# A sequence kernel's front stages rebuilt, and its expert phase issued in another order

## The chip, the cores and the metric

One core of one Trainium2 chip. The metric is device time in microseconds (us) of one execution, lower is better; the value before is a median of three runs. PE is TensorE's matmul stream (PEld its weight loads), DVE is VectorE, ACT ScalarE, POOL GpSimd, and SP SyncE, which issues most transfers.

## The reference

An attention layer with a gated delta rule, then a mixture of experts, each behind a layer norm and with a residual. Shapes: x is 16 x 512 x 256; 16 heads, key width 64, value width 128; 8 experts with an inner width of 32, 2 chosen per token. All in float32.

```python
# attention, x already normed
beta = sigmoid(x @ w_b) * 2
g = -exp(A_log) * softplus(x @ w_a + dt_bias)
q, k, v = (causal_conv_silu(x @ w) for w in (w_q, w_k, w_v))   # 4 taps
q, k = l2norm(q), l2norm(k)
S = S * exp(g_t); delta = (v_t - k_t S) * beta_t                # per step and head
S = S + outer(k_t, delta); o_t = (q_t * DK ** -0.5) S
y = (o * rsqrt(mean(o * o) + 1e-5) * norm_w * silu(x @ w_g)) @ w_out
x = x + layernorm(y)
# experts, on layernorm(x)
V = x @ Wv.T + bv; r = V @ Wg.T + bg; c = sqrt(sum(pv * pv)) / sqrt(8)
s = ln(r) + sigmoid(alpha) * ln(c); w = softmax of the two largest s
x = x + layernorm(V + sum_e w_e * (silu(V @ W1[e].T + b1[e]) @ W2[e].T + b2[e]))
```

## The kernel before

`build` runs these phases in a row; each ends with a barrier of all engines (`Phase.finish`, L102).

1. `make_constants` (L261) builds identity, triangle and block masks on POOL, one instruction after another. PE, DVE and ACT wait for the last of them.
2. `phase_norm` (L315): 16 tiles of 512 tokens. Per tile: load x, statistics (L385), root on POOL (L394), normalize on DVE (L398), eight transposes on PE (L367), two copies on ACT (L375), store to `xT_scratch` (L378), and the gate products with `w_ab` on PE (L341), copied out by DVE (L350). Tiles are staged by one slot each with two buffers.
3. `phase_gates` (L412): loads `w_out`, `norm_w`, `A_log`, `dt_bias`; POOL scales `w_out` (L433) behind clearing the accumulator `acc` (L1142); DVE adds `dt_bias` (L442), ACT takes Abs, Exp and Ln, DVE the maximum (L452) and the product (L454), PE a cumulative sum (L462) and transposes (L472), ACT writes rows (L476), and SP stores them as `g_scratch` and the scaled weights as `wo_scratch`.
4. `phase_delta` (L486): POOL clears and fills `bm`, `m1`, `ktok` (L1106 to L1116), all engines wait for it, then 131 slots. A slot issues stage a (projections, L633, evicted by ACT at L641), stage b (decays: POOL selects from `grow` at L746, ACT takes Exp at L752; inverses) and stage c (recurrence, output, `acc`, L1092) of different blocks. The first 12 slots and the last are written out, the rest is a loop of two slots.
5. `phase_experts` (L1150): 16 tiles of 512 tokens. `body(t)` issues one slot: the steps of all tiles under way, in the order of the table `EXPERT_ORDER` (L74). A name such as `w_T.4` means: step w_T, of the tile that is four slots behind the newest. `issue_slot` (L210) walks the table; each engine gets its own steps in this order and runs them in this order. A step waits for the steps that it reads (`s.need`). After `body(0)`, `compose_weights` (L1249) folds Wv into the router and first expert weights.

The steps of a tile in the experts, in the order of their data:

- x steps: x_bn0, x_mv0, x_ve0 (statistics, L1348, L1326, L1331, DVE), x_rs0 (root, L1334, POOL), x_sh0 (L1337, DVE), x_y1 (normalize, L1316, ACT), x_x1 (residual, L1361, DVE), the same five again as x_bn1 to x_sh1, x_xf (L1316, ACT), x_turn (eight transposes, L1374, PE), x_xT (L1380, ACT).
- q steps: q_mm (router products, L1389, PE), q_b (L1398, DVE), q_sq (ACT), q_c2 (DVE), q_cn (root, L1411, POOL). h steps: h_mm (L1420, PE), h_th, h_z (ACT), h_s (L1434, DVE).
- r steps on DVE: r_sum (L1446), r_cen (L1449), r_cen2, r_var, r_vare, then r_rstd (L1461, POOL), r_n0 (L1465), r_n1, r_score, r_bias. t steps on DVE: t_max, t_idx, t_gap, t_idxf, t_hot, t_den, t_sh0, t_sh1 (L1514), t_w, t_we (L1524), with t_e2 (L1499) on ACT behind t_gap and ahead of t_den.
- w steps: w_turn (L1529, PE), w_T (L1534, ACT), w_V (L1561, PE), w_mm and w_b (L1540, L1545, PE), w_hw (L1551, DVE), w_out (L1567, PE).
- o steps: o_bn (L1573), o_mv, o_ve (DVE), o_rs (POOL), o_sh (DVE), o_n (L1316, ACT), o_sum (L1588, POOL), o_store (SP).

## Time and profile before

| | before |
|---|---|
| median of 3 runs | 5167.19 us (5162.3 to 5168.27) |
| profiled execution, its own time | 5161.75 us |
| its span | 5160.5 us |
| busy: PE, DVE, ACT, POOL | 94%, 81%, 67%, 60% of the span |
| instructions | 151355 |
| DMA | 208.41 MB, mean 40 GB/s |

The span is the time from the first to the last instruction in the profile; the execution's own time is what the runs are measured by. In a timeline row the two numbers at the start are start and duration in us; what stands in brackets is how long the engine had been idle before, and what released it. "x4" means that four instructions are merged in one row. The weight matrices make each float32 product two PE instructions, so a trace counts 16 where the program has 8.

### The profile page before, as it was taken

How to read it: one execution, taken by the hardware profiler on the slowest of the kernel's cores; microseconds unless marked ns; L12 is line 12 of the kernel's file. 1: busy time of each engine (PE TensorE's matmuls, PEld its weight loads, DVE VectorE, ACT ScalarE, POOL GpSimd, SP SyncE). 2: the span in 40 equal slices, each digit the busy share in tenths (PEclk: the TensorE clock that was granted, in tenths of full speed). 3: DMA queues.
4: the chain of work that ended last, by engine and by line, in shares of the span. 5: the costliest groups of instructions: out<-in, count | busy, mean ns of one | idle time of the engine just before them, and what ended most of it. 6: DMA issues, size and time to landing. Idle time of an engine off the chain costs nothing. (4 is left out here: it accounts for less than half of the span.)

```text
span 5160.5 us, 151355 instructions
## 1 busy us (share of the span) xinstructions
PE 4836.9 (94%) x44460; PEld 3853.6 (75%) x44460; DVE 4173.2 (81%) x9991; ACT 3443.0 (67%) x10245; POOL 3110.1 (60%) x4445
## 2 busy tenths in 40 slices
PE   6699999999999999999999999999999999999788
PEld 6477777777777777777777777777777777777566
DVE  5588888888888888888888888888888888887675
ACT  1477776777677776777677767777677777776443
POOL 3566666666666666666666656666566666665465
PEclk9899999999999999999999999999999999999788
DMA  4210111101011010111101111011010110100110
GB/s 147 67 40 32 40 37 39 39 29 43 33 39 39 29 41 36 38 39 33 43 29 39 39 37 39 30 38 45 31 39 30 38 47 29 39 30 20 49 58 33
DMA packets 116478, 208.41 MB, mean 40 GB/s; under 512 B 12418, under 2 KB 70932, under 8 KB 116372
## 3 DMA queue, kind: packets, MB, share of 16 engines
q1 hardware_dynamic: 116372, 207.10, 11.7%
q8 instruction: 53, 0.87, 0.1%
q14 instruction: 53, 0.43, 0.0%
HBM read 187.66 MB, written 19.40 MB: 40 GB/s over the span
## 5 line engine op out<-in xcount | busy, mean ns | idle before, releaser
L648 DVE SCALAR_TENSOR_TENSOR cv<-ps_a,wqkv,cv 128x511 f32<-128x511 f32 (+2 forms) x1536 | 1143.2, 744 | 73.3 <-ACT cv L641 40.1
L633 PE MATMUL ps_a<-xin,wqkv 128*128 128x512 f32 x2048 | 1004.0, 613 | 33.4 <-POOL m L1116 31.1
L852 POOL TENSOR_TENSOR bm<-bat,mask 128x256 f16<-128x256 f32 x1536 | 1032.5, 694 | 0.0
L902 ACT ACTIVATE m<-b 128x256 f16<-128x256 f32 x1536 | 569.2, 388 | 424.7 <-PE b L897 424.6
L913 DVE TENSOR_TENSOR tt<-tt,b 128x256 f16<-128x256 f16 x1536 | 616.0, 415 | 94.8 <-PE b L908 74.5
L955 ACT CAST tt<-bu 128x256 f16<-128x256 f32 x1536 | 572.0, 372 | 134.8 <-PE bu L950 117.1
L1055 POOL TENSOR_TENSOR rms<-msq,epsq 128x2 f32<-128x2 f32 x512 | 99.7, 195 | 920.8 <-ACT sqo L1050 920.8
L633 PEld LDWEIGHTS ps_a<-xin,wqkv 128*128 128x128 f32 x2048 | 363.6, 193 | 292.0 <-issue 285.3
L1087 PE MATMUL ps_a<-wout,yT 128*128 128x256 f32 x2048 | 557.5, 395 | 0.5 <-ACT yT L1081 0.5
L829 DVE SCALAR_TENSOR_TENSOR bat<-ps_a,w,dec 128x256 f32<-128x256 f32 x1024 | 445.3, 476 | 113.7 <-PE ps_a L816 113.7
L897 PEld LDWEIGHTS b<-tt,bm 128*128 128x128 f16 x6144 | 348.8, 98 | 234.6 <-issue 191.8
L780 PE MATMUL ps_b<-wgate,xin 128*128 128x256 f32 x2048 | 504.9, 390 | 0.0
L641 ACT ACTIVATE cv<-ps_a,wqkv 128x512 f32<-128x512 f32 x512 | 352.3, 688 | 174.6 <-PE ps_a L633 174.4
L908 PE MATMUL b<-m,tt 128*128 128x64 f16 x6144 | 421.9, 193 | 32.6 <-ACT m L902 32.5
L950 PE MATMUL bu<-tt,m 128*128 128x64 f16 x6144 | 431.4, 193 | 1.6 <-ACT m L902 0.8
L897 PE MATMUL b<-tt,bm 128*128 128x64 f16 x6144 | 406.3, 193 | 4.4 <-DVE tt L913 3.2
L1092 DVE TENSOR_TENSOR acc<-acc,ps_a 128x256 f32 (+1 forms) x512 | 214.7, 419 | 236.6 <-PE ps_a L1087 235.3
L780 PEld LDWEIGHTS ps_b<-wgate,xin 128*128 128x128 f32 x2048 | 369.5, 190 | 39.1
L816 PE MATMUL ps_a<-kq 64*128 64x256 f32 x2048 | 293.3, 404 | 111.0 <-DVE acc L1092 104.0
L950 PEld LDWEIGHTS bu<-tt,m 128*128 128x128 f16 x6144 | 320.1, 97 | 95.6 <-issue 76.0
L908 PEld LDWEIGHTS b<-m,tt 128*128 128x128 f16 x6144 | 330.2, 98 | 73.7 <-ACT m L902 48.4
L1023 PE MATMUL co<-uu,bat 128*128 128x128 f32 x2048 | 375.2, 275 | 0.0
(223 smaller groups left out, 12447.6 us busy)
## 6 DMA issues: line engine op xcount, KB each, us to landing
xin<-xT_scratch SPq DMA_DIRECT2D x128, 512.0 KB, 3.3
grow<-g_scratch SPq DMA_DIRECT2D x128, 512.0 KB, 4.1
gam<-g_scratch SPq DMA_DIRECT2D x256, 96.0 KB, 2.8
n_x<-in_x SPq DMA_DIRECT2D x16, 512.0 KB, 3.6
xT_scratch<-n_xT SPq DMA_DIRECT2D x16, 512.0 KB, 2.6
e_x<-in_x SPq DMA_DIRECT2D x16, 512.0 KB, 4.2
out_y<-e_yo SPq DMA_DIRECT2D x16, 512.0 KB, 2.9
wqkv<-in_w_qkv SPq DMA_DIRECT2D x32, 128.0 KB, 3.3
```

The costliest lines, as they stand in the source:

```text
L633: ins = pe.matmul(ps[:], wqkv[:, k, j * P:(j + 1) * P], xin[p][:, k, :], start=k == 0, stop=k == KT - 1)
L648: s.done(dve.scalar_tensor_tensor(y[:, r:], ps[:, 0:T - r], tap[:, j, TAPS - 1 - r:TAPS - r], y[:, r:], ALU.mult, ALU.add), f"a_tap{j}{r}")
L780: ins = pe.matmul(ps_b[:, m * 2 * DV:(m + 1) * 2 * DV], xin[p][:, k, t], wg[:, k, :], start=k == 0, stop=k == KT - 1)
L829: ins = dve.scalar_tensor_tensor(bat[:, p:p + 2, u, :], ps[:, n * 2 * P:(n + 1) * 2 * P] .rearrange("p (q t) -> p q t", q=2), col(w1[p], u ...
L852: s.done(pool.tensor_tensor(half_of(bm[:, l, units(g), :], l, 1), half_of(bt[:, units(g), :], l, 1), half_of(c["mask"][:, l, :].unsqueeze( ...
L897: ins = pe.matmul(half_bank(bank, l)[:, k], bm[:, l, u, :], half_of(tt[:, 0], l, 0)[:, u], start=True, stop=True)
L902: s.done(act.mul(half_of(m1[:, l, units(g), :], l, 0), half_bank(bank, l), -1.0), f"b_Me{l}{g}")
L908: ins = pe.matmul(half_bank(bank, l)[:, k], tt[:, 1, u, :], half_of(m1[:, l], l, 0)[:, u], start=True, stop=True)
L913: s.done(dve.tensor_tensor(even, even, half_bank(bank, l), ALU.add), f"b_Ve{l}{g}")
L950: ins = pe.matmul(half_bank(bu, l)[:, k], m1[:, l, u, :], half_of(tt[:, 1], l, 1)[:, u], start=True, stop=True)
L955: s.done(act.copy(half_of(tt[:, 1, units(g), :], l, 1), half_bank(bu, l)), f"b_Ue{l}{g}")
L1087: ins = pe.matmul(ps_a[m % 2][:, 0:D], yT[:, h, :], wo[:, h, :], start=h == 0, stop=h == 1)
```

## The change

- `make_constants` builds only identity, `still`, `half` and `minus_half` at once; the rest, with `bm`, `m1` and `ktok` for delta, comes from a generator that `phase_norm` advances by three steps a slot (`n_build`).
- `phase_norm` is written as steps with lags (`NORM_ORDER`), with four x and xT buffers, two for the others; normalizing goes from DVE to ACT. It also loads `A_log`, `dt_bias`, `norm_w` and `w_out`, scales `w_out` on POOL in eight parts, and stores `wo_scratch` at its end.
- `phase_gates` is gone. Its arithmetic is `decay_gates` in `phase_delta`, in buffers of delta; the first loads of delta are issued ahead of it (`load_first`), the loads of `grow` and `gam` wait for `g_scratch`, which is stored in two halves from ACT's queue.
- `acc` isn't cleared; the first 16 blocks copy into it. 20 delta slots are written out before the loop, not 12.
- `EXPERT_ORDER` is another list, with lags 0 to 3 (19 slots) in place of 0 to 5 (21 slots), and two waits of PE for steps of PE are added.

```diff
--- before.py
+++ after.py
 
 EXPERT_ORDER = """
-    w_turn.4 w_T.4 x_bn0 h_th0.3 w_V0.4 o_sum.5 l_x x_x1.1 w_V1.4 h_s1.4 h_z0.3 x_mv0 x_bn1.1 h_th1.3 h_s0.3
-    r_sum.3 r_cen.3 r_cen2.3 r_var.3 x_ve0 h_z1.3 w_mm.4 r_vare.3 x_xf.2 r_rstd.3 w_hw0.4 w_hw1.4 x_mv1.1 x_rs0
-    x_turn.2 r_n0.3 x_ve1.1 r_n1.3 w_out0.4 r_score.3 x_sh0 r_bias.3 w_out1.4 t_max.3 x_xT.2 o_bn0.4 t_idx.3
-    o_bn1.4 q_mm.2 x_y1 o_store.5 h_mm0.2 t_gap.3 t_idxf.3 o_mv.4 q_b.2 t_e2.3 o_ve.4 q_sq.2 x_rs1.1 t_hot.3
-    t_den.3 t_sh0.3 o_rs.4 q_c2.2 h_mm1.2 t_sh1.3 o_sh.4 t_w.3 o_n0.4 x_sh1.1 q_cn.2 o_n1.4 t_we.3
+    o_bn0.3 o_bn1.3 o_mv.3 o_ve.3 o_rs.3 o_sh.3 o_n0.3 o_n1.3 o_sum.3 o_store.3 t_max.2 t_idx.2 t_gap.2 t_idxf.2
+    t_e2.2 t_hot.2 t_den.2 t_sh0.2 t_sh1.2 t_w.2 t_we.2 w_turn.2 w_V0.2 w_V1.2 w_T.2 w_mm.2 w_hw0.2 w_hw1.2
+    w_out0.2 w_out1.2 q_mm.1 q_b.1 h_mm0.1 h_mm1.1 q_sq.1 h_th0.1 h_z0.1 h_th1.1 h_z1.1 q_c2.1 q_cn.1 h_s0.1 h_s1.1
+    r_sum.1 r_cen.1 r_cen2.1 r_var.1 r_vare.1 r_rstd.1 r_n0.1 r_n1.1 r_score.1 r_bias.1 l_x x_bn0 x_mv0 x_ve0 x_rs0
+    x_sh0 x_y1 x_x1 x_bn1 x_mv1 x_ve1 x_rs1 x_sh1 x_xf x_turn x_xT
 """.split()
...
+    def build_later():
+
+
...
+            step(pool.memset(c["m1"][:, lev, 0, :], 0.0))
+            odd = lambda t: t.rearrange("p u (b k r) -> p u b k r", k=2, r=2 << lev)[:, :, :, 1, :]
+            step(pool.tensor_copy(odd(c["m1"][:, lev, 0:1, :]), odd(c["ident16"][:].unsqueeze(1))))
+            yield
+            step(pool.tensor_copy(c["m1"][:, lev, 1:NU, :], c["m1"][:, lev, 0:1, :].broadcast_to([P, NU - 1, P])))
+            yield
+        for p in range(2):
+            step(pool.memset(c["ktok"][p][:], 0.0))
+            yield
+
     step(pool.memset(c["ident"][:], 1.0))
     step(pool.affine_select(out=c["ident"][:], in_=c["ident"][:], pattern=[[-1, P]], compare_op=ALU.is_equal,
                             fill=0.0, base=0, channel_multiplier=1))
...
+NORM_ORDER = """
+    n_load n_sh.3 n_xT.4 n_bn.2 n_xn.3 n_mv.2 n_ve.2 n_rs.2 n_store.4 n_turn.3 n_ab.4 n_build n_abo.5
+""".split()
+N_LAG = lags_of(NORM_ORDER)
+N_LAGS = max(N_LAG.values())
+BUILD = 3
+
...
+        def loads_later(t):
+
+
+            if t == 0:
+                sp.dma_start(wab[:], w_ab).then_inc(s.sem("n_wab_in"), 16)
...
+        def tile(i):
+            p, q = i % 2, i % NX
+            if (yield "n_load"):
+                s.need(sp, i - NX, "n_xn")
+                s.loaded(sp.dma_start(x_in[q][:], x[i:i + 1].rearrange("a p c d -> p (a c) d")), f"n_x_in{q}")
+            if (yield "n_bn"):
+                dve.wait_ge(s.sem(f"n_x_in{q}"), (i // NX + 1) * 16)
+                s.need(dve, i - 1, "n_mv")
+                for k in range(CH):
+                    ins = dve.bn_stats(stats[:, k, :], x_in[q][:, k, :])
+                s.done(ins, "n_bn")
+            if (yield "n_mv"):
+                s.need(dve, i, "n_bn")
+                s.need(dve, i - 1, "n_sh")
+                settle(dve, c["still"][:, 0:2])
+                for k in range(CH):
+                    ins = dve.bn_aggr(mv[:, k, :], stats[:, k, :])
+                s.done(ins, "n_mv")
+            if (yield "n_ve"):
+                s.need(dve, i, "n_mv")
+                s.need(dve, i - 2, "n_xn")
+                s.done(dve.tensor_scalar(rstd[p][:], mv[:, :, 1], LN_EPS, None, ALU.add), "n_ve")
+            if (yield "n_rs"):
+                s.need(pool, i, "n_ve")
+                s.done(pool.tensor_tensor(rstd[p][:], rstd[p][:], c["minus_half"][:, 0:CH], ALU.pow), "n_rs")
+            if (yield "n_sh"):
+                s.need(dve, i, "n_rs")
...
+                s.need(act, i - 2, "n_turn")
+                for k in range(CH):
+                    ins = act.activation(xn[p][:, k, :], x_in[q][:, k, :], ACT.Identity, bias=shift[p][:, k:k + 1],
+                                         scale=rstd[p][:, k:k + 1])
+                s.done(ins, "n_xn")
+            if (yield "n_turn"):
+                s.need(pe, i, "n_xn")
+                s.need(pe, i - 2, "n_xT")
                 for k in range(KT):
                     for m in range(CH):
...
+                s.need(act, i - NX, "n_ab")
+                if i >= NX:
+                    act.wait_ge(s.sem(f"n_xT_out{q}"), (i // NX) * 16)
                 for k in range(KT):
...
+        def build(t):
+            if (yield "n_build"):
+                for k in range(BUILD):
+                    next(later, None)
+                if t >= NB // 2:
+                    next(scaling, None)
+
+        for t in range(NB + N_LAGS):
+            loads_later(t)
+            threads = [(build(t), 0)]
+            for lag in range(N_LAGS + 1):
+                if active(t - lag, NB):
+                    threads.append((tile(t - lag), lag))
+            issue_slot(N_LAG, threads)
+        for k in later:
+            pass
+        for k in scaling:
+            pass
+        sp.wait_ge(s_ws, NP)
+        sp.dma_start(wo_dram.rearrange("n p h d -> p n (h d)"), wo[:]).then_inc(s_small, 16)
+        for q in range(NX):
+            sp.wait_ge(s.sem(f"n_xT_out{q}"), 16 * NB // NX)
+        sp.wait_ge(s_small, 48)
         ctx.finish()
...
@@ -1089,7 +1094,11 @@
                 if (yield f"c_acc{m}"):
                     s.need(dve, i, f"c_out{m}")
                     a = acc[:, bass.ds((i % NB) * CH + m, 1), :].rearrange("p a d -> p (a d)")
-                    s.done(dve.tensor_tensor(a, a, ps_a[m % 2][:, 0:D], ALU.add), f"c_acc{m}")
+                    if isinstance(i, int) and i < NB:
+                        ins = dve.tensor_copy(a, ps_a[m % 2][:, 0:D])
+                    else:
+                        ins = dve.tensor_tensor(a, a, ps_a[m % 2][:, 0:D], ALU.add)
+                    s.done(ins, f"c_acc{m}")
 
             return [recur()] + [emit(m) for m in range(CH)]
 
-        zero = s.sem("zeroed")
-        pool.memset(bm[:], 0.0).then_inc(zero, 1)
-        pool.memset(m1[:], 0.0).then_inc(zero, 1)
-        pool.memset(still[:], 0.0).then_inc(zero, 1)
-        for p in range(2):
-            pool.memset(ktok[p][:], 0.0).then_inc(zero, 1)
-        pool.wait_ge(zero, 5)
-        for l in range(NLEV):
-            odd = lambda t: t.rearrange("p u (b k r) -> p u b k r", k=2, r=2 << l)[:, :, :, 1, :]
-            ident = c["ident16"][:].unsqueeze(1)
-            for u in range(NU):
-                ins = pool.tensor_copy(odd(m1[:, l, u:u + 1, :]), odd(ident))
-        ins.then_inc(zero, 1)
-        for eng in (pe, act, dve, pool):
-            eng.wait_ge(zero, 6)
-        load_pair(0)
...
+        def load_first():
+
+
+            load_x(0, 0, 0)
+            pair = w_qkv[0:1].rearrange("a p n -> p (a n)")
+            for j in range(4):
+                s.loaded(sp.dma_start(wqkv[:, :, j * P:(j + 1) * P],
+                                      pair[:, 0:KT * N_QKV].rearrange("p (k n) -> p k n", k=KT)[:, :, j * P:(j + 1) * P]),
+                         f"wqkv_in{j}")
+            s.loaded(sp.dma_start(wq[:, KT * N_QKV:], pair[:, KT * N_QKV:]), "tap_in")
+            load_x(1, 1, 1)
+            s.loaded(sp.dma_start(wg[:], w_gate[0:1].rearrange("a p k n -> p (a k) n")), "wg_in")
+            s.loaded(sp.dma_start(wo[:], wo_dram[0:1].rearrange("a p h d -> p (a h) d")), "wo_in")
+            sp.wait_ge(s_out, 32)
+            load_rows(0)
+            load_rows(1)
+            load_x(2, 2, 0)
...
+        def decay_gates():
+
+
+            W = NIT * NU
+            z, az = [tinv[k][:].rearrange("p u t -> p (u t)") for k in range(2)]
+            rows = vtok[0][:]
+            ps = halves
+            at0, at1 = gate_tok[0][:, 0:W], gate_tok[1][:, 0:W]
+            by_head = lambda t: t.rearrange("p (q x h) -> p q x h", q=NP, h=2)
+            spread = lambda t: t.rearrange("p (q x h) -> p q x h", x=1, h=2).broadcast_to([P, NP, W // H, 2])
+            s_v, s_a, s_p = ctx.semaphore("g_dve"), ctx.semaphore("g_act"), ctx.semaphore("g_pe")
+
+            dve.tensor_tensor(by_head(z), by_head(at0), spread(dtb[:]), ALU.add).then_inc(s_v, 1)
+            act.wait_ge(s_v, 1)
...
+            act.activation(az, z, ACT.Abs).then_inc(s_a, 1)
+            act.wait_ge(s_a, 1)
+            act.activation(az, az, ACT.Exp, scale=-1.0).then_inc(s_a, 1)
+            act.activation(alog[:], alog[:], ACT.Exp).then_inc(s_a, 1)
+            act.activation(at1, at1, ACT.Tanh, scale=0.5).then_inc(s_a, 1)
+            act.wait_ge(s_a, 2)
+            act.activation(az, az, ACT.Ln, bias=1.0).then_inc(s_a, 1)
+            dve.wait_ge(s_v, 1)
+            dve.wait_ge(s_a, 5)
+            dve.scalar_tensor_tensor(z, z, 0.0, az, ALU.max, ALU.add).then_inc(s_v, 1)
+            dve.wait_ge(s_v, 2)
+            dve.tensor_tensor(by_head(z), by_head(z), spread(alog[:]), ALU.mult).then_inc(s_v, 1)
+            pe.wait_ge(s_v, 3)
+            for k in range(2):
+                pe.matmul(ps[k][:], c["upper"][:], z[:, k * 512:(k + 1) * 512], start=True, stop=True).then_inc(s_p, 1)
+            dve.tensor_scalar(at1, at1, 1.0, None, ALU.add).then_inc(s_v, 1)
+            for k in range(2):
+                dve.wait_ge(s_p, k + 1)
...
+                act.dma_start(g_dram[k * 512:(k + 1) * 512].rearrange("(a r) t -> r a t", r=P),
+                              rows[:, 4 * k:4 * k + 4, :]).then_inc(s_out, 16)
+            act.wait_ge(s_v, 6)
+            pe.wait_ge(s_a, 7)
+            dve.wait_ge(s_a, 7)
+            pool.wait_ge(s_a, 7)
+            pool.wait_ge(s_v, 6)
+
+        load_first()
         with sp.Fori(1, NP) as hp:
             load_pair(hp)
-        in_slots(nc, NIT, LAGS, 12, COMPUTE, body)
+        decay_gates()
+        in_slots(nc, NIT, LAGS, FIRST, COMPUTE, body)
         ctx.finish()
 
 
...
@@ -1533,7 +1604,7 @@
                 s.need(act, i - 1, "w_b")
                 s.done(act.copy(weT[:], rb[:]), "w_T")
             if (yield "w_mm"):
-                s.need(pe, i, "w_T")
+                s.need(pe, i, "w_T", "w_V1")
                 free(pe, i, "w_mm")
                 for m in range(KT):
                     at = m * HALF
@@ -1561,7 +1632,7 @@
                         ins = pe.matmul(o[j], xT[p][:, k, tok[j]], wv[:, k, :], start=k == 0, stop=False)
                 s.done(ins, f"w_V{half}")
             if (yield f"w_out{half}"):
-                s.need(pe, i, "w_hw0", "w_hw1")
+                s.need(pe, i, "w_hw0", "w_hw1", "w_b")
                 for j in range(2):
                     for k in range(KT):
                         ins = pe.matmul(o[j], hw[p][:, k, tok[j]], w2[:, k, :], start=False, stop=k == KT - 1)
```

What the table moves is seen on two engines, each in one expert slot of the steady state. First DVE, from t_we (L1524) on, in the kernel before:

```order
L1524 TENSOR_TENSOR e_we<-e_hot 128x8x8
L1348 BN_STATS e_stats<-acc 128x6 x4
L1361 TENSOR_TENSOR acc<-acc,e_x 128x1024
L1434 SCALAR_TENSOR_TENSOR e_hw<-e_hth,e_hz 128x512
L258 TENSOR_TENSOR e_still<-e_still 1x1
L1326 BN_AGGR e_mv<-e_stats 128x2 x4
L1348 BN_STATS e_stats<-acc 128x6 x4
L1434 SCALAR_TENSOR_TENSOR e_hw<-e_hth,e_hz 128x512
L1446 TENSOR_REDUCE e_total<-e_rv 128x8
L1449 SCALAR_TENSOR_TENSOR e_rv<-e_rv,e_total 128x64
L1452 TENSOR_TENSOR e_cen<-e_rv 128x64
L1455 TENSOR_REDUCE e_var<-e_cen 128x8
```

and in the changed kernel, where t_we is L1595, t_sh1 L1585, w_hw L1622, q_b L1469 and L1470, q_c2 L1478, h_s L1505 and r_sum L1517:

```order
L1582 RECIPROCAL e_share<-e_share 128x4
L1585 TENSOR_TENSOR e_share<-e_share,e_e 128x4
L1589 TENSOR_TENSOR e_hot<-e_hot,e_share 128x32 x2
L1595 TENSOR_TENSOR e_we<-e_hot 128x8x8
L1622 TENSOR_TENSOR e_hw<-e_hw,e_t 128x512 x2
L1469 TENSOR_TENSOR e_rv<-e_rb,e_rowb 128x4x8
L1470 TENSOR_TENSOR e_pv<-e_rb,e_rowb 128x256
L1478 TENSOR_REDUCE e_c<-e_pv 128x32
L1505 SCALAR_TENSOR_TENSOR e_hw<-e_hth,e_hz 128x512 x2
L1517 TENSOR_REDUCE e_total<-e_rv 128x8
```

Between t_we and w_hw there stood thirteen rows of other steps; now none does, and none between w_hw and q_b. PE in one slot, before (w_turn L1529, w_V L1561, w_mm L1540, w_b L1545, x_turn L1374, w_out L1567, q_mm L1389, h_mm L1420):

```order
L1529 MATMUL e_rb<-ident,e_we 128x128 x4
L1561 MATMUL e_ob<-e_wv,e_xT 128x256 x8
L1540 MATMUL e_t<-e_weT,e_spread 128x512 x2
L1545 MATMUL e_ob<-e_b2v,e_weT 128x256 x4
L1374 MATMUL e_t<-ident,e_xf 128x128 x8
L1567 MATMUL e_ob<-e_w,e_hw 128x256 x8
L1389 MATMUL e_rb<-e_wrx,e_xT 128x72 x8
L1420 MATMUL e_t<-e_xT,e_w1x 128x512 x4
```

and in the changed kernel (the same steps at L1600, L1632, L1611, L1616, L1638, L1460, L1491 and L1445):

```order
L1600 MATMUL e_rb<-ident,e_we 128x128 x4
L1632 MATMUL e_ob<-e_wv,e_xT 128x256 x8
L1611 MATMUL e_t<-e_weT,e_spread 128x512 x2
L1616 MATMUL e_ob<-e_b2v,e_weT 128x256 x4
L1638 MATMUL e_ob<-e_w,e_hw 128x256 x8
L1460 MATMUL e_rb<-e_wrx,e_xT 128x72 x8
L1491 MATMUL e_t<-e_xT,e_w1x 128x512 x4
L1445 MATMUL e_t<-ident,e_xf 128x128 x8
```

x_turn moved from between w_b and w_out to the end of the slot. The tiles that the rows belong to differ too: before, q_mm and h_mm were of the tile two behind the newest and w steps of the one four behind; now they are one and two behind, and x_turn is of the newest.

## Rows read from the trace of the kernel before

**Rows 1.** Busy time by stretch: norm (0 to 110 us), experts (4787 us on)
```profile
0.00:110.00 110.00, 83.37 (x384) 81.32 (x384) 66.19 (x352) 18.46 (x33) 25.53 (x54) 1.00 0.44 153
...
4787.00:5161.00 374.00, 304.33 (x1312) 228.14 (x1312) 252.56 (x1185) 170.13 (x347) 207.64 (x112) 0.81 0.14 48
```

**Rows 2.** Timeline of the norm: start us, duration us, engine, line, operation, idle before
```profile
12.17 1.40 DVE L385 BATCH_NORM_STATS2 n_stats<-n_x 128x6 f32<-128x256 f32 x4 [12.17 <-POOL first L311]
...
17.00 1.94 PE L367 MATMUL n_turn<-ident,n_xn 128*128 128x128 f32 x8 [17.00 <-DVE n_xn L398]
...
99.19 1.97 PE L367 MATMUL n_turn<-ident,n_xn 128*128 128x128 f32 x8
```

**Rows 3.** Timeline of the decay gates, same columns
```profile
119.45 1.22 DVE L442 TENSOR_TENSOR g_z<-gate_tok,g_dtb 128x1024 f32<-128x1024 f32 x1 [9.74 <-DMA g_dtb<-in_dt_bias]
...
124.69 3.69 POOL L433 TENSOR_SCALAR g_wo<-g_wo,g_normw 128x4096 f32<-128x4096 f32 x1
...
125.51 3.93 DVE L452 SCALAR_TENSOR_TENSOR g_z<-g_z,g_az 128x1024 f32<-128x1024 f32 x1 [4.83 <-ACT g_az L449]
...
136.34 0.60 ACT L476 ACTIVATE g_rows<-g_ps 128x512 f32<-128x512 f32 x1 [0.31 <-PE g_ps L472]
```

**Rows 4.** DMA issues up to 180 us: count, KB each, median us to landing
```profile
wo_scratch<-g_wo SPq DMA_DIRECT2D x1, 2048.0 KB, 8.6
...
grow<-g_scratch SPq DMA_DIRECT2D x2, 512.0 KB, 4.6
```

**Rows 5.** Timeline of the first delta slot
```profile
167.39 6.74 PE L633 MATMUL ps_a<-xin,wqkv 128*128 128x512 f32 x8 [31.09 <-POOL m L1116]
...
171.83 1.26 ACT L752 ACTIVATE dec<-dec,gate_tok 128x128 f32<-128x128 f32 x4
```

**Rows 6.** Timeline of two expert slots: q_cn on GpSimd
```profile
4916.36 5.42 POOL L1411 TENSOR_TENSOR e_rv<-e_c,half 128x32 f32<-128x32 f32 x1
...
4936.89 5.42 POOL L1411 TENSOR_TENSOR e_rv<-e_c,half 128x32 f32<-128x32 f32 x1
```

**Rows 7.** Timeline of the experts: o_sum on GpSimd and r_cen on VectorE
```profile
4901.18 2.82 POOL L1588 TENSOR_TENSOR e_yo<-e_yo,acc 128x1024 f32<-128x1024 f32 x1
...
4901.95 2.13 DVE L1449 SCALAR_TENSOR_TENSOR e_rv<-e_rv,e_total 128x64 f32<-128x64 f32 x1
...
4830.50 0.22 DVE L1449 SCALAR_TENSOR_TENSOR e_rv<-e_rv,e_total 128x64 f32<-128x64 f32 x1
```

**Rows 8.** Timeline of the experts: first norms of a tile (x steps)
```profile
4806.47 1.40 DVE L1348 BATCH_NORM_STATS2 e_stats<-acc 128x6 f32<-128x256 f32 x4 [14.25 <-POOL e_rowb L1303]
...
4810.84 2.02 POOL L1334 TENSOR_TENSOR e_rstd<-e_rstd,minus_half 128x4 f32<-128x4 f32 x2 [4.47 <-DVE e_rstd L1331]
...
4812.20 2.07 ACT L1316 ACTIVATE acc<-acc,e_shift,e_rstd 128x256 f32<-128x256 f32 x4 [7.63 <-DVE e_shift L1337]
...
4918.32 1.21 DVE L1361 TENSOR_TENSOR acc<-acc,e_x 128x1024 f32<-128x1024 f32 x1
```

**Rows 9.** The last tile's t_we, w_V, w_hw and w_out, and the clock beside w_V
```profile
5137.39 0.23 DVE L1524 TENSOR_TENSOR e_we<-e_hot 128x64 f32<-128x64 f32 x1
...
5138.58 5.99 PE L1561 MATMUL e_ob<-e_wv,e_xT 128*128 128x256 f32 x16
...
5145.68 1.28 DVE L1551 TENSOR_TENSOR e_hw<-e_hw,e_t 128x512 f32<-128x512 f32 x2 [7.46 <-PE e_t L1540]
...
5147.02 3.72 PE L1567 MATMUL e_ob<-e_w,e_hw 128*128 128x256 f32 x16 [0.52 <-DVE e_hw L1551]
...
5136.60:5143.20 6.60, 5.53 (x15) 4.62 (x16) 1.20 (x5) 2.40 (x5) 2.70 (x2) 0.50 0.13 53
```

**Rows 10.** Timeline of expert slot 2: q_b, r_sum and r_n0 on VectorE
```profile
4823.21 0.19 DVE L1398 TENSOR_TENSOR e_rv<-e_rb,e_rowb 128x32 f32<-128x32 f32 x1 [4.70 <-PE e_rb L1389]
...
4830.24 0.22 DVE L1446 TENSOR_REDUCE e_total<-e_rv 128x8 f32<-128x64 f32 x1 [0.87 <-POOL e_rv L1411]
...
4833.19 0.23 DVE L1465 TENSOR_TENSOR e_rv<-e_rv,e_var 128x64 f32<-128x64 f32 x1 [1.40 <-POOL e_var L1461]
```

More of the change, by code:

```diff
@@ new lines, in make_constants @@
+    step(pool.memset(c["ident"][:], 1.0))
+    step(pool.affine_select(out=c["ident"][:], in_=c["ident"][:], pattern=[[-1, P]], compare_op=ALU.is_equal,
+                            fill=0.0, base=0, channel_multiplier=1))
+    step(pool.memset(c["still"][:], 0.0))
+    for name, value in (("half", 0.5), ("minus_half", -0.5)):
+        step(pool.memset(c[name][:], value))
+    later = build_later()
+    next(later)
+    return c, s_const, n[0], later
+NORM_ORDER = """
+    n_load n_sh.3 n_xT.4 n_bn.2 n_xn.3 n_mv.2 n_ve.2 n_rs.2 n_store.4 n_turn.3 n_ab.4 n_build n_abo.5
@@ L353, in body @@
[L353 to L364 removed]
+        s.series("n_dve", ["n_bn", "n_mv", "n_ve"])
@@ L523, in phase_delta @@
         kqs = two("kqs", [P, 2, REST, P])
-        ktok = two("ktok", [P, REST, 4, DK])
+        ktok = c["ktok"]
         vtok = two("vtok", [P, NU, DV])
@@ L538, in phase_delta @@
         sqo = sb("sqo", [P, 2, DV], F16)
-        still = sb("still", [P, 6])
         msq, rms = sb("msq", [P, NU]), sb("rms", [P, NU])
```

284 lines of the change are left out of this document (110 added, 174 removed).

## Prediction

> **What bounds the kernel now.** First I split the span into its stages [rows 1]. The stretch 0 to 110 us is the norm, up to 147 us the decay gates, up to 167 us the filling of delta's buffers, then some 4,620 us of delta steps, and from 4787 us the experts, 374 us long. The change leaves the delta steps almost as they are, so only about 167 us in front and 374 us behind are at stake. I read each of these as a chain of waits, since a stage's busy shares say nothing about what an order of steps does to it.
>
> The front is a row of stages that don't overlap. VectorE's first statistics wait until GpSimd has built its last constant, at 12.17 us; the first transposes start at 17.00 us and the last of the 16 tiles at 99.19 us, so a tile takes 82.19 / 15 = 5.48 us [rows 2]. PE is busy 83.37 us in that stretch [rows 1], 5.2 us a tile: the norm is bound by PE. The gates wait until 119.45 us for `dt_bias`, which is queued behind 2 MB of `w_out`; the maximum at 125.51 us takes 3.93 us since it stands behind GpSimd's scaling of `w_out` until 128.38 us; the last rows are evicted at 136.94 us [rows 3]. Then `wo_scratch` lands 8.6 us after its issue [rows 4], and PE starts the first projection at 167.39 us, 31 us idle, released by GpSimd's last mask [rows 5].
>
> The experts run in slots. The root of the router norms (q_cn) starts at 4916.36 and again at 4936.89 us, so a slot is 20.5 us [rows 6]. It is short because five lags and an interleaved order let every wait of one tile be covered by work of others: of 374 us PE is busy 304 [rows 1].
>
> **The change, the front.** Constants: five instead of 30-odd stand before the norm, so its start waits for the first x tile, not for GpSimd. That tile is SP's second issue; with 4.6 us for 512 KB [rows 4] it is there by 6 us. Statistics 1.4, aggregation and root some 2.3, one table load of 1.3 and the four activations of 2.07 (the form of [rows 8]) put the first transposes at about 12 us, 5 us earlier. The lags can only remove the 5.48 - 5.2 us a tile that PE idles, and the end (last gates products) comes to about 102.5 us. The last store and then `wo_scratch` are issued at about 97 us and landed by 106, so the next phase begins at 107, with `dt_bias` already there: 12.5 us before 119.45. All masks, bm, m1 and ktok are written beside the norm, some 3 steps a slot of at most 1 us each, on a GpSimd that is busy 25.53 of 110 us [rows 1]: nothing, and if that cover were too small the rest would come behind the norm at its own length. Inside the gates Tanh moves ahead of Ln (+1.06) and GpSimd no longer holds the maximum (-2.7): -1.6 us. What stood between the last rows at 136.94 and the first projection at 167.39 goes, but a new wait comes: grow can be loaded only once g_scratch has landed. Two transfers of up to 4.6 us [rows 4], their issues of 0.4, the select and a table load, each some 1.2, put the first Exp of dec some 12 us behind the rows; it stood 4.4 us behind PE's start (171.83 against 167.39 [rows 5]) and ScalarE queues the next eviction behind it. I take 6 us of PE's 30.4 as lost so: -24.4. Front in all: 12.5 + 1.6 + 24.4 = 38.5 us saved. Eight more written-out delta slots and a copy in place of an add for the first 16 blocks I cost at nothing: together they touch 16 of 131 slots of 35 us, on which even 1% is 5 us.
>
> **The change, the experts.** The two added waits (w_V1, w_b) are on PE for work earlier on PE: nothing. The order is another matter. The new list is the order of one tile's own steps, oldest tile first, with three lags. On VectorE the reader sees t_we directly ahead of w_hw, and w_hw directly ahead of q_b; PE has w_turn, w_V, w_mm, w_out, q_mm in one piece between them. So each engine waits where it hands over. I walk VectorE's slot by rows:
> - X, first norms of the newest tile: statistics 1.40, settle, aggregate and add 0.7, root and handoffs 1.3, x_y1 2.1, x_x1 1.2 [rows 8], and statistics, aggregation, root again 3.4: 10.1 us. x_y1 and both roots stand open.
> - OT: ScalarE still has x_xf 2.07, must wait for eight transposes (1.97 in [rows 2]), copy twice 0.6 [rows 3], and then normalize the oldest tile, 2, before it comes to t_e2 0.2: with handoffs 7.7 us, more than the 5 us that VectorE has for o_bn to t_hot. In the same moment GpSimd starts o_sum, which reads SBUF for some 2.4 us (2.82 in [rows 7], where an operation of VectorE was still ahead of it). [Rows 7] show what that does: r_cen took 2.13 us beside o_sum, and 0.22 us when GpSimd was idle; its end is o_sum's end. The step t_sh1, also a two-input operation from SBUF, I take to be held the same way, 1.75 us. With the last t steps 1.1: 10.5 us.
> - W: t_we, w_turn, w_V, w_mm, both w_hw. The last tile of the present trace has just this chain alone: from the end of t_we at 5137.62 to the end of w_hw at 5146.96, 9.3 us [rows 9].
> - Q: w_out 3.72 [rows 9], q_mm some 1.9 and handoffs: 5.8 us.
> - C: from q_b at 4823.21 over q_sq, q_c2 and q_cn to r_sum at 4830.24 [rows 10]: 7.0 us. h_s fits inside.
> - R: r_sum at 4830.24 to r_n0 at 4833.19 [rows 10] and four steps of 0.24: 3.9 us. r_cen now costs 0.22.
>
> Sum: 10.1 + 10.5 + 9.3 + 5.8 + 7.0 + 3.9 = 46.6 us a slot, against 20.5. Slot 0 has X, 3 us for its x tile, transposes and then the composed weights (the 14.25 us idle of [rows 8] less the 2 of x_y1): 29.5. Slot 1 (q_mm at the lower clock, C, R, X) 24.8, slot 2 42.8, slots 3 to 15 13 x 46.6 = 605.8, slot 16 (no X) 36.5, slot 17 21.7, slot 18 9.8. In all 771 us against 373: +398 us.
>
> The Trainium skill, SBUF — State Buffer, section Who interferes with whom, says that a VectorE instruction with two SBUF inputs blocks against a GpSimd instruction that reads SBUF, whoever is first. By that rule t_sh1 is held as I have it. By its letter q_cn would hold too, h_s and all. The trace disagrees for that one: x_x1, two SBUF inputs, starts at 4918.32 us inside q_cn and takes 1.21 us [rows 6, 8].
>
> **Sum.** 5160.5 - 38.5 + 398 = 5520 us of span; the profiled execution's own time is 1.25 us above its span: 5521. That execution lies 5.4 us under the median of the three runs, 0.1%; I leave it there. Forecast 5521 us, 6.9% slower.
>
> **Rivals.**
> 1. *The lower clock stays through w_out and q_mm.* After an idle stretch PE came back at 0.50: the granted clock was 0.50 while w_V took 5.99 us in the tail, and w_out, the same 16 forms, took 3.72 after it [rows 9]. PE will idle about 25 of 47 us in each slot. If w_out and q_mm also ran at half the rate, a slot would grow by up to 3.5 us, 16 times: 5577 us. The Trainium skill, TensorE: Matmul & The Clock Gate, section What's actually happening, has the array at 1.2 GHz by default and released by activity; the trace agrees, and it leaves open how much of each burst is paid.
> 2. *Nothing is held and PE recovers at once.* Without the 1.75 us at t_sh1 the total is 5521 - 15 x 1.75 = 5495; with w_V at w_out's 3.72 us as well, in 16 slots, 5459. For it: t_sh1 has four elements. Against it: [rows 7] show a small operation held.
> 3. *q_cn does hold h_s*, which then costs its 1.3 us behind it in 17 slots: 5543. Against it speaks x_x1 above.
> 4. *The front doesn't deliver*: the reader of the rows waits, or `w_out`'s 2 MB delay the third x tile so that the norm gains nothing. Half of 38.5 us is lost: 5540.
> 5. *The other side, faster.* The slot stays bound by PE, since every engine has other tiles' steps to run at each handoff; then 19 slots instead of 21 and the front give 5161.75 - 38.5 - 2 x 20.5 = 5082 us. It decides below a slot of 25 us (46.6 x (373 + 38.5) / 771). Against it: each engine's order is fixed, and the six open handoffs above stand in it next to each other.
>
> **How the numbers follow.** Forecast with terms as above 0.57; rival 1 0.15; rival 2 0.15; rival 3 0.04; rival 4 0.07; rival 5 0.02. The range takes in rivals 1 to 4 and the bounds of W and Q: 5455 to 5585 us. A measurement of this kernel tells about 0.2% (10 us) from no change; only rival 5 is faster, and nothing lands within 10 us of 5167: faster 0.02, same 0.01 (for a case between that I don't see), slower 0.97.
>
> **What would show it.** Experts' slot near 46.6 us, with VectorE idle behind w_mm, behind q_mm and behind q_cn, and PE idle over 20 us a slot; t_sh1 at about 2 us if it is held; r_cen at 0.22 us. First projection near 129 us, with ScalarE waiting for dec after its first eviction; delta slots unchanged. A slot under 40 us, or a front that ends after 145 us, would make the prediction wrong.

## The result

The changed kernel takes 5506.01 us (median of 4 runs, 5500.14 to 5512.49), the kernel before 5165.05 us beside it: a ratio of 1.066, 95% interval 1.0642 to 1.0679. It is slower by 341 us. The forecast was 5521 us, 5455 to 5585. The profiled execution's own time is 5503.28 us, its span 5502.1 us.

First the busy time of two stretches of the profile after, the front and the experts (us, then busy time of PE, PE's weight loads, DVE, ACT and POOL, the granted clock, DMA share and GB/s). They answer to [rows 1].

```profile
0.00:101.00 101.00, 81.89 (x384) 81.29 (x384) 40.43 (x209) 49.98 (x97) 46.01 (x86) 1.00 0.56 209
...
4739.00:5502.00 763.00, 319.94 (x1312) 234.84 (x1312) 284.14 (x1185) 173.51 (x347) 203.70 (x112) 0.68 0.07 24
```

The experts have the same 1312 matmul instructions, but 763 us instead of 374. PE is busy 42% of it, was 81%. Both sides of the sum are there: the experts begin at 4739.4 us, 48.1 us sooner than before (4787.5), and last 762.7 us, 389.7 us longer than the 373.0 before.

**The front**, from the timeline of the profile after (answers to [rows 2, 3, 5]):

```profile
4.91 1.41 DVE L402 BATCH_NORM_STATS2 n_stats<-n_x 128x6 f32<-128x256 f32 x4 [4.91 <-DMA n_x<-in_x]
...
11.99 0.87 PE L434 MATMUL n_turn<-ident,n_xn 128*128 128x128 f32 x3 [11.99 <-POOL mask L295]
...
88.38 1.97 PE L434 MATMUL n_turn<-ident,n_xn 128*128 128x128 f32 x8
...
100.90 1.23 DVE L1153 TENSOR_TENSOR tinv<-gate_tok,g_dtb 128x1024 f32<-128x1024 f32 x1 [3.50 <-PEq L105]
...
107.83 1.23 DVE L1164 SCALAR_TENSOR_TENSOR tinv<-tinv 128x1024 f32<-128x1024 f32 x1 [5.71 <-ACT tinv L1161]
...
116.81 3.70 PE L638 MATMUL ps_a<-xin,wqkv 128*128 128x512 f32 x8 [1.12 <-ACT vtok L1182]
...
123.17 1.10 POOL L751 TENSOR_SCALAR_AFFINE_SELECT dec<-grow 128x1024 f32<-128x1024 f32 x1
...
124.30 1.28 ACT L757 ACTIVATE dec<-dec,gate_tok 128x128 f32<-128x128 f32 x4 [3.39 <-POOL dec L751]
```

Statistics start when the first x tile has landed. The bracket at 11.99 us names a mask of GpSimd, but in the kernel the first transposes wait for n_xn, which ScalarE ended at 11.84 us. The norm's pace is (88.38 - 11.99) / 15 = 5.09 us a tile, the gates' first operation stands at 100.90 us (before 119.45), the maximum takes 1.23 us (before 3.93), and the first projection starts at 116.81 us (before 167.39). The first products of q and k come at 139.7 us, before at 187.9: 48.2 us saved. From there to the experts it is 4,600 us in both.

**One expert slot**, same columns. The list moves every step, so these rows answer to [rows 6 to 10].

```profile
5146.24 1.40 DVE L1419 BATCH_NORM_STATS2 e_stats<-acc 128x6 f32<-128x256 f32 x4
...
5156.34 1.42 DVE L1644 BATCH_NORM_STATS2 e_stats<-e_ob 128x6 f32<-128x256 f32 x4
...
5163.58 2.34 POOL L1659 TENSOR_TENSOR e_yo<-e_yo,acc 128x1024 f32<-128x1024 f32 x1 [4.05 <-ACT e_yo L1387]
5163.63 2.32 DVE L1579 TENSOR_SCALAR e_share<-e_e 128x4 f32<-128x4 f32 x1 [2.21 <-ACT e_e L1570]
...
5166.72 0.22 DVE L1595 TENSOR_TENSOR e_we<-e_hot 128x64 f32<-128x64 f32 x1
...
5167.90 4.82 PE L1632 MATMUL e_ob<-e_wv,e_xT 128*128 128x256 f32 x16
...
5173.99 1.28 DVE L1622 TENSOR_TENSOR e_hw<-e_hw,e_t 128x512 f32<-128x512 f32 x2 [7.05 <-PE e_t L1611]
...
5175.33 3.72 PE L1638 MATMUL e_ob<-e_w,e_hw 128*128 128x256 f32 x16 [0.51 <-DVE e_hw L1622]
...
5180.83 0.19 DVE L1469 TENSOR_TENSOR e_rv<-e_rb,e_rowb 128x32 f32<-128x32 f32 x1 [5.55 <-PE e_rb L1460]
...
5182.33 5.44 POOL L1482 TENSOR_TENSOR e_rv<-e_c,half 128x32 f32<-128x32 f32 x1 [16.41 <-DVE e_c L1478]
...
5187.87 0.22 DVE L1517 TENSOR_REDUCE e_total<-e_rv 128x8 f32<-128x64 f32 x1 [1.57 <-POOL e_rv L1482]
5188.12 0.22 DVE L1520 SCALAR_TENSOR_TENSOR e_rv<-e_rv,e_total 128x64 f32<-128x64 f32 x1
...
5191.67 0.42 DVE L1419 BATCH_NORM_STATS2 e_stats<-acc 128x6 f32<-128x256 f32 x1
```

Read on VectorE from the statistics at 5146.24 to the same at 5191.67 the slot falls into the prediction's six pieces: X 10.1 us, OT 10.6, W 8.3 (to the end of w_hw at 5175.27), Q 5.6, C 7.0, R 3.8; 45.4 us in all. The slots on either side take 46.5 and 46.6 us; their w_V takes 5.85 and 5.98 us instead of 4.82. In two of the 16 slots w_out is slow too:

```profile
5081.94 5.21 PE L1638 MATMUL e_ob<-e_w,e_hw 128*128 128x256 f32 x16 [0.51 <-DVE e_hw L1622]
```

From store to store, 14 of them, the mean is (5443.74 - 4841.92) / 13 = 46.3 us.

VectorE's waits over twelve such slots say the same (waited for, total us, times, longest):

```profile
DVE e_hw L1622 <- PE e_t L1611: 92.9, 12, 8.3
DVE e_rv L1469 <- PE e_rb L1460: 69.6, 12, 7.0
DVE e_shift L1408 <- POOL e_rstd L1405: 41.4, 37, 1.1
DVE e_hw L1505 <- ACT e_hz L1501: 34.7, 26, 1.6
DVE acc L1432 <- ACT acc L1387: 27.8, 13, 2.1
DVE e_share L1579 <- ACT e_e L1570: 26.5, 12, 2.2
DVE e_rv L1536 <- POOL e_var L1532: 22.7, 13, 1.8
DVE e_total L1517 <- POOL e_rv L1482: 20.4, 13, 1.6
DVE e_c L1478 <- ACT e_pv L1474: 5.8, 12, 0.5
```

No single wait is to blame: nine kinds of hand-over, each 0.5 to 8 us at a time, add up to 342 us, some 28 us a slot. The row of o_sum at 5163.58 beside that of t_den at 5163.63 is the one surprise. The held step is there and costs 2.15 us, where 1.75 were forecast, but it is t_den, an operation on four elements with one input tensor, and not t_sh1.

### The profile page after: what moved, and what is told of

Same layout as the page of the kernel before. It is cut to its first block and busy times, and to the rows that moved or that the text cites. A ratio compares the mean times of both kernels' runs of the same rounds, so it can differ in the third digit from the quotient of the medians.

```text
span 5502.1 us, 150332 instructions
## 1 busy us (share of the span) xinstructions
PE 4848.4 (88%) x44460; PEld 3857.0 (70%) x44460; DVE 4175.0 (76%) x9847; ACT 3480.0 (63%) x10309; POOL 3092.9 (56%) x4422
## 5 line engine op out<-in xcount | busy, mean ns | idle before, releaser
L653 DVE SCALAR_TENSOR_TENSOR cv<-ps_a,wqkv,cv 128x511 f32<-128x511 f32 (+2 forms) x1536 | 1143.1, 744 | 45.7 <-ACT cv L646 12.5
L1063 POOL TENSOR_TENSOR rms<-rms,minus_half 128x2 f32<-128x2 f32 x512 | 360.3, 704 | 20.2
```

What stands on the lines that cost most here:

```text
L653: s.done(dve.scalar_tensor_tensor(y[:, r:], ps[:, 0:T - r], tap[:, j, TAPS - 1 - r:TAPS - r], y[:, r:], ALU.mult, ALU.add), f"a_tap{j}{r}")
```

## Experiments

Twelve kernels. Ratios are to the kernel before on the same chip, with 95% intervals. The kernel before took between 5161 and 5168 us beside the various runs, so differences of a few us between the times of two experiments aren't told here; the ratios and the traces decide there.

### 1 and 2. The list alone, and everything but the list

```
 e1: changed kernel, EXPERT_ORDER = the list of before
 e2: kernel before,  EXPERT_ORDER = the new list, and
-                s.need(pe, i, "w_T")
+                s.need(pe, i, "w_T", "w_V1")
-                s.need(pe, i, "w_hw0", "w_hw1")
+                s.need(pe, i, "w_hw0", "w_hw1", "w_b")
```

> The changed kernel with the list of expert steps of before; norm, gates, delta and the two added waits as changed. Theory (the list alone costs the time, and the front keeps what it gained): the experts' stretch goes from 762.7 us back to 373, within 3; the milestone at the first kq products stays near 139.7 us and the experts start near 4739 us. Time 5506 - 390 = 5116 us, between 5106 and 5128. Rival (part of the loss lies in the two added waits on TensorE, or in the front's larger constants that the delta steps and experts share SBUF with): experts over 380 us or delta longer, time over 5130 us.

> The kernel before with the new list of expert steps and the two waits that go with it, everything else as before. Theory (loss and gain don't touch each other): experts 763 us, front as before, time 5165 + 390 = 5555 us, between 5543 and 5567. Rival (the two parts interact, for instance through where memory lies): more than 12 us off 5555.

Measured: e1 5118.72 us, ratio 0.9905 (0.9888 to 0.9922); e2 5556.78 us, ratio 1.0757 (1.0739 to 1.0775). Here is the experts' stretch of e1, then of e2.

```profile
4749.40:5122.50 373.10, 304.38 (x1312) 229.69 (x1312) 252.40 (x1185) 170.00 (x347) 208.03 (x112) 0.81 0.14 48
```
```profile
4789.00:5554.00 765.00, 320.84 (x1312) 235.74 (x1312) 284.10 (x1184) 173.52 (x347) 203.42 (x112) 0.68 0.07 24
```

e1's experts are the 373 us of before, with the two added waits in them; e2's run from 4788.7 to 5553.9 us, 765 us, within 3 us of the changed kernel's. Both theories hold, and the two halves add up: list +389 us, front -48 us. The front's gain is real and the list gives it back eight times. (e1's experts begin at 4749.4 us although its first q and k products come at 139.2: the delta steps of that one execution were 10 us longer, 0.2%, which is what single executions differ by here.)

### 3. o_sum where it holds nothing

```
             if (yield "o_sum"):
                 s.need(pool, i, "o_n1")
+                if i + 1 < NB:
+                    s.need(pool, i + 1, "t_we")
```

> The changed kernel, where o_sum on GpSimd also waits for t_we of the next tile, so that it runs beside w_turn, w_V and w_mm instead of beside t_den. Theory (o_sum's operation holds t_den, a tensor_scalar of four elements per partition, for 2.15 us, and that lies on the path): t_den takes 0.17 us, each of 15 slots is 2.1 us shorter, time 5506 - 32 = 5474 us, between 5466 and 5482. Rival (the hold only covers a wait that ends as late, for ScalarE's t_e2 or for TensorE's clock): t_den short but the slot unchanged, 5506 us within 6. Second rival (o_sum then holds w_hw instead): w_hw over 2 us, time 5506 or more.

Measured: 5479.77 us, ratio 1.0609 (1.0591 to 1.0626). The same step in e3's timeline:

```profile
5199.37 0.17 DVE L1579 TENSOR_SCALAR e_share<-e_e 128x4 f32<-128x4 f32 x1 [2.21 <-ACT e_e L1570]
```

t_den takes 0.17 us and the slot 44.4 us (46.3 less 1.9). The time falls by 26 us and lies inside the interval given. The hold is shown, and that it lies on the path. It isn't the full 32 us because PE's clock took a part: w_V now takes 5.9 us in all slots but the last (granted clock 0.61 beside it), while six slots of the changed kernel had one of 4.7 to 4.9 us; in return w_out takes 3.72 us throughout. The prediction had read only half of the rule in the Trainium skill, SBUF — State Buffer, section Who interferes with whom. Beside two-input instructions it names `tensor_scalar` as one that can, where its operands meet certain conditions, enter a mode that takes VectorE's shared port pair too and so contends with GpSimd. By that part t_den can be held as well as t_sh1, and the first to meet o_sum pays; the trace agrees, 2.32 us against 0.17.

### 4. Building the constants ahead of the norm

The kernel of e1 with `for k in later: pass` ahead of the norm's loop.

> The kernel of e1 (changed kernel with the list of before), with all the masks and buffers built on GpSimd ahead of the norm instead of beside it. In the changed kernel's trace these operations take some 24 us of GpSimd. Theory (building beside the norm hides them wholly, on a GpSimd that is otherwise half idle there): the norm's first root is needed at about 7 us and now comes at about 27, so all that follows is 20 us later: 5118.7 + 20 = 5139 us, between 5130 and 5146. Rival (they weren't free beside the norm: they slowed its other engines' reads, and without them a tile is faster): norm pace under 5.0 us a tile, time under 5128 us.

Measured: 5137.65 us, ratio 0.995 (0.9933 to 0.9967), 19 us over e1. PE's transposes of the norm in e4 (min/median/max ns, first and last start in us):

```profile
L434 PE MATMUL n_turn<-ident,n_xn x128: 421/421/476, 33.8 to 111.8; 128*128 128x128 f32 x128
```

They start at 33.8 us instead of 12, and span 78 us as in the changed kernel: at this pace of the norm the work beside it was free. The theory holds, for this norm; e10 shows where it ends.

### 5 and 9. TensorE kept busy ahead of w_turn

```
+            if (yield "w_junk"):
+                free(pe, i, "w_turn")
+                for j in range(20):
+                    ins = pe.matmul(rb[:, 0:D], xT[p][:, j % 2, 0:P], wv[:, j % 2, :], start=True, stop=True)
+                s.done(ins, "w_junk")
             if (yield "w_turn"):
```

> The changed kernel with 20 more matmuls a slot on TensorE right ahead of w_turn, of the form of w_V, into the bank that w_turn then overwrites, so that TensorE works where it sat idle for 6.4 us. Theory (w_V pays for the idle time ahead of it with a lower clock: 4.82 us, while w_out, the same 16 forms, takes 3.72 us): w_V takes 3.7 to 3.9 us, slot about 1.1 us shorter, 16 times: 5506 - 18 = 5488 us, between 5480 and 5497. Rival (w_V's length comes from something else than the idle time): 5506 within 6. Second rival (the extra work runs into t_we's end): 5512 or more.

Measured: 5535.17 us, ratio 1.0723 (1.0705 to 1.0741). The second rival, and a slip of mine: each float32 product is two instructions, so the filler was twice as long as meant. The filler ran 3.0 us past the end of t_we, w_V fell to 3.62 us, and w_out took 5.2 to 5.4 us in every second slot. e9 has `range(10)`.

> The kernel of e5 with half its filler: 10 matmuls, which the trace shows as 20 instructions. In e5 the filler was 40 instructions, took 9.77 us and put w_turn 3.0 us behind t_we, while w_V fell to 3.62 us. Theory (the filler ends ahead of t_we now, and w_V stays short): w_V 3.6 to 3.9 us, time 5506 - 16 x 1.1 = 5488 us, between 5480 and 5497. Rival (TensorE needs the unbroken work of e5 to be fast at w_V): w_V 4.5 us or more, time 5506 within 6.

Measured: 5481.94 us, ratio 1.062 (1.0604 to 1.0637). PE's timeline in e9, from the filler on:

```profile
5192.63 5.98 PE L1599 MATMUL e_rb<-e_wv,e_xT 128*128 128x256 f32 x20
5199.29 0.66 PE L1605 MATMUL e_rb<-ident,e_we 128*128 128x128 f32 x4 [0.68 <-DVE e_we L1595]
5199.78 3.62 PE L1637 MATMUL e_ob<-e_wv,e_xT 128*128 128x256 f32 x16
...
5206.01 5.33 PE L1643 MATMUL e_ob<-e_w,e_hw 128*128 128x256 f32 x16 [0.51 <-DVE e_hw L1627]
```

w_V takes 3.62 us in every slot but the last (5.57), and 44.3 us is the mean slot: useless work makes the kernel 24 us faster (21 us by the ratios). It gains more than 18 because w_V had taken 5.6 to 6.0 us in ten of the 16 slots. But in every third slot, five in all, w_out now takes 5.3 us instead of 3.72; in the changed kernel it was two. The granted clock is 1.00 beside w_V and 0.69 beside the slow w_out. So filler took the lower clock off the burst behind it, and more of it fell on a later one. What decides on which burst it falls wasn't tested.

### 7. Values ahead of the weights' transposes

On the kernel of e3; only PE's order changes.

```
-    ... t_we.2 w_turn.2 w_V0.2 w_V1.2 w_T.2 ...
+    ... t_we.2 w_V0.2 w_V1.2 w_turn.2 w_T.2 ...
```

> The kernel of e3, with w_V0 and w_V1 put ahead of w_turn in the list; on TensorE alone anything moves. Theory (W is a chain of w_turn, w_T, w_V, w_mm, in which w_V needs nothing of the routing and stands in it only by its place): w_V starts when o_n is done, about 5 us before t_we ends less its own 4.8 us, and w_hw comes 3.6 us earlier in each of 16 slots: 5479.8 - 57 = 5423 us, between 5412 and 5440. Rival (a lower clock for the rest of the burst eats part): 5440 to 5465 us.

Measured: 5447.76 us, ratio 1.0554 (1.0536 to 1.0572), 32 us under e3 and not 57. PE in e7, and the granted clock (third number from the end) beside its w_out:

```profile
5178.01 5.09 PE L1632 MATMUL e_ob<-e_wv,e_xT 128*128 128x256 f32 x16 [2.17 <-ACT e_yo L1387]
...
5186.73 5.41 PE L1638 MATMUL e_ob<-e_w,e_hw 128*128 128x256 f32 x16 [0.52 <-DVE e_hw L1622]
```
```profile
5186.70:5192.20 5.50, 5.47 (x19) 4.55 (x20) 0.00 (x0) 0.00 (x0) 0.00 (x0) 0.69 0.01 3
```

w_hw waits 5.6 us for w_mm on average (13 waits, 73.0 us) instead of 8.1, so 2.5 us of the 3.6 came. In every second slot w_out gives 1.7 us back at a mean clock of 0.69, 0.8 us a slot. What is left is 1.7 us, and the mean slot falls from 44.4 to 42.7 us. The rival is what happened.

### 6 and 12. More lags, then the groups in other places

e6 keeps the groups whole and oldest first, but with five lags:

```
+    h_th0.3 ... h_s1.3 o_bn0.5 ... o_store.5 w_turn.4 ... w_out1.4 r_sum.3 ... r_bias.3 t_max.3 ... t_we.3
+    x_xf.2 x_turn.2 x_xT.2 q_mm.2 ... q_cn.2 x_bn1.1 ... x_sh1.1 l_x x_bn0 ... x_x1
```

> The changed kernel with the same whole groups of steps, oldest tile first, but with five lags instead of three: first norm 0, second 1, transposes, router and hidden products 2, gates of the hidden part and all routing 3, weights and outputs 4, last norm and sum 5. The groups are not interleaved with each other. Theory (what costs is that one tile's steps hand over between engines next to each other within one slot; with a slot between the hand-overs each engine finds finished work): slot falls from 46.3 to some 24 to 30 us, 21 slots, experts about 550 us, time about 5290 us, between 5220 and 5400. Rival (the fine interleaving of the old list is what hides the waits, lags by themselves give little): slot over 38 us, time over 5500 us.

Measured: 5447.11 us, ratio 1.0543 (1.0525 to 1.056); slot 42.8 us. The theory fell, and of the rival its slot came true but not its time of over 5500 us: five lags by themselves bring 3.5 of 46.3 us. The longest of e6's waits on PE, over 15 slots:

```profile
PE e_ob L1633 <- ACT e_yo L1388: 206.7, 15, 17.1
```

w_V waits 14 us a slot for o_n, since the four banks `ob` are not free until the tile before is normalized, and that stood one slot behind w_out. The lags had opened hand-overs between engines and stretched the time that a buffer is held. e12 puts the groups by that (`h.3` stands for the h steps with lag 3, and so on):

```
+    h.3 w_turn.4 ... w_mm.4 r.3 t.3 w_hw.4 w_out.4 x_xf.2 x_turn.2 x_xT.2 x_bn1.1 ... x_sh1.1
+    l_x x_bn0 ... x_x1 o_bn0.4 ... o_sh.4 q_mm.2 ... q_cn.2 o_n0.4 o_n1.4 o_sum.4 o_store.4
```

> The kernel of e6 with its groups placed by what waited in it: the last norm's statistics in the slot of w_out, behind the routing and the x norms, o_n at the end of the slot; w_hw behind the routing; transposes ahead of the x norms. In e6 TensorE waited 15.8 us a slot for o_n of the tile before, since the output banks were held until the next slot. Theory (in e6 that wait set the slot of 38.6 us, and the slot falls to what VectorE's own chain takes, 28 to 32 us): time about 5506 - 763 + 21 x 30 = 5373 us, between 5320 and 5430. Rival (another loop of the same length stands behind it): slot over 36 us, time over 5440 us.

Measured: 5272.35 us, ratio 1.0218 (1.0203 to 1.0234); slot (5179.65 - 4841.50) / 11 = 30.7 us. Experts' stretch of e12:

```profile
4741.00:5271.00 530.00, 305.42 (x1312) 219.53 (x1312) 274.25 (x1185) 167.54 (x347) 203.32 (x112) 0.80 0.10 34
```

The slot is as forecast, though the expectation misread e6: its slot was 42.8 us, not 38.6, and its mean wait 13.8 us, where 15.8 was a long one. The time is 48 us under the low end, since I counted 21 full slots where the first and last are short. So 60% of the loss goes (234 of 390 us) with groups that are nearly whole. That fits the view that it counts how much stands between a group and what it waits for; but e12 moves several groups at once, and what each is worth wasn't run. The granted clock is back at 0.80. This list is still worse than the old one, whose slot is 20.4 us.

### 8 and 10. What bounds the norm

e8 leaves out half of the norm's gate products (`for k in range(1)`), e10 also moves n_xn ahead of n_xT:

```
-    n_load n_sh.3 n_xT.4 n_bn.2 n_xn.3 n_mv.2 ...
+    n_load n_sh.3 n_xn.3 n_xT.4 n_bn.2 n_mv.2 ...
```

> The kernel of e1, with half of the norm's gate products left out (one of the two contraction blocks; the output is not the reference's). Theory (the norm is bound by TensorE, 73.3 us busy of 76.4): 8 of 16 matmuls of 0.216 us go from each tile, pace from 5.09 to some 3.5 us, front 24 us shorter: 5118.7 - 24 = 5095 us, between 5087 and 5103. Rival (DMA, at 0.56 of its share, or the hand-overs between the engines bound it as much): pace over 4.7 us, time over 5112 us.

> The kernel of e8 (half of the norm's gate products left out, so not the reference's output) with n_xn put ahead of n_xT in the list of the norm's steps, so that ScalarE normalizes the next tile before it waits for the transposes of the last. Theory (e8 kept its pace of 5.09 us because a loop of three, transposes 1.97, eviction 1.07 and normalizing 2.08 us, is as long as TensorE's own work, and the order on ScalarE closes it): the loop opens, pace falls to about 3.5 us, TensorE's or ScalarE's own work, time 5116.7 - 15 x 1.5 = 5094 us, between 5086 and 5103. Rival (DMA bounds the norm): pace over 4.7 us, over 5110 us.

Measured: e8 5116.73 us, ratio 0.9915 (0.9898 to 0.9931); e10 5099.99 us, ratio 0.9878 (0.9862 to 0.9893). PE's wait in e8's norm, then its transposes in e10.

```profile
PE n_turn L434 <- ACT n_xn L426: 23.7, 14, 3.1
```
```profile
L434 PE MATMUL n_turn<-ident,n_xn x128: 417/421/477, 12.1 to 72.5; 128*128 128x128 f32 x128
```

e8 missed: PE has 22 us less to do, waits 23.7 us for n_xn where the changed kernel's trace has 3.1, and the pace stays 5.09 us. PE, busy 96% of the changed kernel's norm, was only one of two bounds of about the same length. The other is the ring of transposes 1.97, eviction 1.07 and normalizing 2.08 us, closed by ScalarE's order. e10 opens it, and the mean pace falls to 3.9 us. Less work for PE alone was worth nothing, with the other order it brings 17 us more; the other order alone, with all products, wasn't run.

The mean of 3.9 us hides two paces. From 20.7 to 34.1 us a tile takes 3.36 us, from 37.9 to 64.2 us 4.38. GpSimd's copies and its scaling of `w_out` stand beside VectorE's small operations there:

```profile
41.45 0.93 POOL L326 COPY m<-m 128x896 f16<-128x896 f16 x1
41.48 0.91 DVE L258 TENSOR_TENSOR still<-still 1x1 f32<-1x1 f32 x1
...
42.49 0.69 POOL L387 TENSOR_SCALAR n_wo<-n_wo,n_normw 128x512 f32<-128x512 f32 x1
42.71 0.49 DVE L414 TENSOR_SCALAR n_rstd<-n_mv 128x4 f32<-128x4 f32 x1
```

Each ends with GpSimd's operation; undisturbed they took 0.15 and 0.17 us. So the rival of e4, that building slows the norm's other engines, is seen as soon as nothing longer covers it: about 1 us a tile. No run of this norm without the work beside it was made.

### 11. The products the other way round

```
+    n_load n_sh.3 n_xn.3 n_xT.4 n_bn.2 n_mv.2 n_ve.2 n_rs.2 n_store.4 n_abT.5 n_turn.3 n_ab.4 n_abc.4 n_build n_abo.5
...
+                for k in range(KT):
+                    ins = pe.matmul(abh[p][0:2 * H, :], wab[:, k, :], xT[q][:, k, :], start=k == 0, stop=k == KT - 1)
...
+                s.done(dve.tensor_copy(abs_[p][0:2 * H, :], abh[p][0:2 * H, :]), "n_abc")
...
+                    ins = pe.transpose(ab[p][:, m, 0:2 * H], abs_[p][0:2 * H, m * P:(m + 1) * P],
+                                       c["ident"][0:2 * H, 0:2 * H])
```

> The kernel of e1 with the norm's list as in e10 and with the gate products the other way round: w_ab as weights and the 512 columns of xT streamed, 4 instructions in place of 16 a tile, then a copy on VectorE and four transposes back; all outputs as the reference has them. It is the attempt at a faster version. Theory (TensorE's 16 instructions of 0.216 us were mostly loading of weights, and the loop of e8 is open): a tile takes transposes 1.97, products 4 x 0.46 to 0.71 and transposes 0.6 to 1.0 us, some 4.4 us in place of 5.09: 5118.7 - 10 = 5108 us, between 5093 and 5119. Rival (the other way round costs as much at the rate at which TensorE runs in the norm): pace 4.9 us or more, 5115 to 5130 us.

Measured: 5153.06 us (11 runs), ratio 0.9981 (0.9972 to 0.999): 34 us over e1, past even the rival. One tile in e11:

```profile
61.67 3.62 PE L455 MATMUL n_abh<-n_xT,n_wab 128*32 128x512 f32 x4
...
65.33 0.68 DVE L460 COPY n_abs<-n_abh 32x512 f32<-32x512 f32 x1 [5.73 <-PE n_abh L455]
...
66.20 0.14 DVE L423 SCALAR_TENSOR_TENSOR n_shift<-n_mv,n_rstd 128x4 f32<-128x4 f32 x1
...
66.38 2.07 ACT L428 ACTIVATE n_xn<-n_x,n_shift,n_rstd 128x256 f32<-128x256 f32 x4 [5.71 <-DVE n_shift L423]
```

In this tile the four instructions take 3.62 us, no less than the sixteen did. The clock makes the difference: in another tile, at 54.43 us, they take 1.90 us. The granted clock (third number from the end) beside them, there and here:

```profile
54.45:56.30 1.85, 1.85 (x5) 0.34 (x4) 0.00 (x0) 0.00 (x0) 1.67 (x4) 1.00 0.63 248
61.70:65.25 3.55, 3.55 (x5) 0.51 (x4) 0.00 (x0) 0.00 (x0) 2.05 (x4) 0.50 0.81 275
```

And the new copy stands ahead of n_sh on VectorE, so normalizing waits for the products: a new ring, copy, n_sh, n_xn, transposes, products. It takes 6.4 us in the tile at full clock, 8.7 in the one shown, 7.5 on average, so even at full clock it is longer than the 5.09 us of e1. I had priced the operation and not asked what stands behind it.

Of the kernels that compute all of the reference e1 is the fastest: 0.9905 of before.

## Why the prediction was right

The sign, the cause and the size were right. The time lies 15 us under 5521. By its steps:

- **Front, 38.5 us forecast, 48.2 measured.** By its terms: up to the gates' first operation 12.5 forecast, 18.6 measured. First transposes at 12 us were right (11.99), but the end at 102.5 us stands for 5.4 us a tile and it was 5.09, which is 4.7 us over 15 tiles. Part of that is a slip in the sum: its own terms, 5 us sooner and 0.28 us less a tile, take the end from 108.9 us to 99.7, not to 102.5. The floor of 5.2 divided the busy time of 110 us by 16 and was too high. That the norm is bound by PE was half of it: e8 shows a ring of the same length. Gates 1.6 forecast, 1.6 measured, with the maximum at 1.23 us. Last rows to the first projection: 30.4 saved as forecast. I took 6 us of it as lost to the wait for dec; ScalarE waits 3.4 us, and by the first q and k products 2.4 us are lost. So "near 129 us" for the first projection was also booked at the wrong place: the loss comes behind it, and it starts at 116.8. That building beside this norm costs nothing is shown by e4.
- **Added waits at nothing.** Shown by e1, whose experts take 373.1 us with them.
- **Experts' slot 46.6 us: 46.3.** X, OT, C and R are right within 0.1 us, OT by luck: t_e2 ended after 7.3 us, not 7.7, and the hold was 0.4 us longer. W, 9.3 us, was taken from the tail, where w_V took 5.99 us at a clock of 0.50. That fits the ten slots where w_V took 5.6 to 6.0 us, and is 1 us too long in the six where it took 4.7 to 4.9. Q was 0.2 us too long, and 1.2 too short in the two slots with a slow w_out. The errors of W and Q partly cancel in the mean.
- **The hold by o_sum, 1.75 us at t_sh1.** The size was near (2.15 us at t_den, 1.9 us off the slot in e3), the step wrong. t_den stands two steps earlier and met o_sum first; t_sh1 took 0.16 us.
- **Stretch 771 us: 763.** Four of the eight us are 13 slots of 0.3, the rest lies in the short slots at the ends.
- **Rival 1**, lower clock through w_out and q_mm: false as a rule of the changed kernel, where 14 of 16 w_out took 3.72 us and q_mm 1.90. But two w_out took 5.21 us at a clock of 0.70, and e7 and e9 show more of them one edit away.
- **Rival 2**, nothing held and PE recovers at once: false on both counts. e3 without the hold is 26 us faster, e9 with a fast w_V 24 us, each net of what the clock took elsewhere.
- **Rival 3**, q_cn holds h_s: false; h_s took 0.69 us inside q_cn. **Rival 4**, the front doesn't deliver: false. **Rival 5**, slot bound by PE: false; PE idles 26 us of 46.

The deviations add up: front -10 us, experts -8 us, and +3 us from the profiled execution to the median give 5506.

## What to carry to other kernels

To price an order of steps, walk the engine with the most hand-overs through one slot, piece by piece, with durations from rows; busy shares would have said nothing here, and the walk came out within 1%, with small errors of both signs in it. When steps are moved or given more lag, ask two things of each engine: what stands directly behind the waiting step (e8, e11), and which buffer is now held longer (e6). An engine that is 96% busy need not be the bound: a ring of other work of the same length hides every gain there until it is opened too. And what is free beside a slow stage has to be priced again when the stage gets faster (e4, e10).

## What the runs showed of the hardware

- A `tensor_scalar` of four elements a partition, with one SBUF input, took 2.32 us beside GpSimd's 128x1024 `tensor_tensor` and 0.17 us without it (e3). A `tensor_tensor` of one element took 0.91 us beside a copy of GpSimd in f16, and 0.15 us without (e10). GpSimd's 5.44 us root of 32 elements did not hold h_s, two SBUF inputs of 512, which took 0.69 us inside it.
- After idle time of PE the lower clock showed in some burst behind it, and not always in the first: with w_V made fast by filler (3.62 us), w_out took 5.3 us in every third slot; with w_V moved ahead, 5.41 in every second.
- 16 instructions that stream 32 columns took 3.46 us a tile in the norm; the same product as 4 that stream 512 columns took 3.62 us at a granted clock of 0.50 and 1.90 us at 1.00 (e11).
- The clock in the record may be wrong at the start of a trace. It is 1.00 through the norm of the changed kernel, but the eight transposes take 1.97 us there, as they do in e11 at 0.50; in e11 at 1.00 they take 1.09 us, at 53.41 us. By these durations, though by nothing else, PE ran at the lower level in the norm.
